# An S4 and mixture-of-experts block: filter tables made in 16 wide steps, expert chunks regrouped, and the last stage's loads issued by SyncE

## What is computed

```python
# s4: a long convolution per feature h, whose kernel comes from 64 complex modes
dtA  = exp(log_dt)[:, None] * A                       # [H, 64]
coef = C * (exp(dtA) - 1.0) / A
vand = exp(dtA[:, :, None] * arange(Lq))              # powers of exp(dtA)
kern = 2.0 * einsum('hn,hnl->hl', coef, vand).real    # [H, 4096]
y = irfft(rfft(xn) * rfft(kern))[:Lq]
z = gelu(y + xn * D) @ W_out + b_out                  # gated by a sigmoid half
# moe: 16 experts, every token through all, weighted by `combine` (2 nonzero of 16)
h  = silu(xn @ We1[e] + be1) * (xn @ We3[e] + be3)
yo = h @ We2[e] + be2
out = sum_e combine[:, e] * yo_e  +  shared expert
```

## Time and profile before

| | us |
|---|---|
| median of 2 runs | 10923.64 |
| the two runs | 10829.25 and 11018.03 |
| the profiled execution | 10848.99 |
| its span (core 5, the slowest) | 10847.4 |
| PE busy, of the span | 4786.6 (44%) |
| DVE busy | 4317.1 (40%) |
| ACT busy | 2336.4 (22%) |
| POOL busy | 2228.4 (21%) |

### The profile page before, as it was taken

The page is one execution under the profiler, slowest core; times in us unless marked ns, Lnnn a source line. Parts: engine busy times, 40 slices in busy tenths (PEclk is TensorE's granted clock), DMA queues, the critical chain, the costliest instruction groups (busy, mean ns, idle before and its releaser), DMA issues.

```text
span 10847.4 us, 92715 instructions; the slowest of 8 cores (10731.5 to 10847.4 us)
## 1 busy us (share of the span) xinstructions
PE 4786.6 (44%) x26752; PEld 2699.4 (25%) x26752; DVE 4317.1 (40%) x9126; ACT 2336.4 (22%) x3389; POOL 2228.4 (21%) x3656
## 2 busy tenths in 40 slices
PE   0000556666565555555433333323315554544541
PEld 0000222232222222222211111111114343433431
DVE  6244344444433343344355555544413232322322
ACT  1021333333333333333333333311100000000000
POOL 1000222333232223233222222200101111111110
PEclk9999777777777777777655555557657777777776
DMA  4500222222222222221111111110073435445347
GB/s 131 117 15 13 53 53 53 56 57 56 58 58 55 53 52 61 53 53 45 39 28 27 27 28 27 27 43 26 23 98 71 67 75 68 70 67 70 70 70 179
DMA packets 471658, 620.67 MB, mean 57 GB/s; under 512 B 285073, under 2 KB 330513, under 8 KB 470114
## 3 DMA queue, kind: packets, MB, share of 16 engines
q0 software_dynamic: 223152, 513.42, 23.4%
q1 hardware_dynamic: 144034, 75.11, 2.9%
q10 hardware_dynamic: 103968, 26.22, 1.5%
HBM read 389.99 MB, written 259.13 MB: 60 GB/s over the span
## 4 chain that ended last, share of the span: by engine, by line
PE 32%; DVE 24%; DMA 13%; ACT 10%; issue 8%; another core or an unknown queue 6%; POOL 4%; DVEq 1%; ACTq 1%; SPq 0%; POOLq 0%
PE PS L1363 9%; PE PS L1368 9%; PE PS L1550 8%; DMA p_h<-dH 5%; POOL dKLOC L920 3%; DVE p_h L1568 3%; PE PS L538 2%; DMA dH<-p_h 2%; DMA dKLOC<-p_xbuf 2%; ACT L1074 2%; ACT L548 2%; PE PS L1028 1%; DMA dP<-p_at 1%; DVEq L187 1%
## 5 line engine op out<-in xcount | busy, mean ns | idle before, releaser
L1550 PE MATMUL PS<-p_h,p_w 128*128 128x256 bf16 x8192 | 1142.8, 312 | 1226.2 <-DVE p_h L1574 1226.2
L1550 PEld LDWEIGHTS PS<-p_h,p_w 128*128 128x128 bf16 x8192 | 904.9, 112 | 1464.2 <-issue 1258.8
L1363 PE MATMUL PS<-xnF,p_w 128*128 128x512 bf16 x4608 | 1150.5, 395 | 102.0 <-ACT p_h L1391 102.0
L1368 PE MATMUL PS<-xnF,p_w 128*128 128x512 bf16 x4608 | 1096.3, 381 | 0.0
L1568 DVE SCALAR_TENSOR_TENSOR p_h<-p_h,sb_be_t,p_s 128x256 bf16<-128x256 bf16 x1024 | 496.0, 484 | 1157.9 <-DMA p_h<-dH 1072.1
L920 POOL DMA_DIRECT2D dKLOC<-p_xbuf x1024 | 599.1, 763 | 1615.6 <-ACT p_xbuf L552 1601.8
L561 DVE TENSOR_TENSOR p_tw<-p_gbuf,s_t1r 128x512 bf16<-128x512 bf16 x128 | 54.4, 425 | 2029.0 <-ACT p_gbuf L549 2029.0
L1499 POOL DMA_DIRECT2D p_s<-dS x272 | 206.0, 757 | 2211.4 <-PE PS L1550 2211.4
L538 PE MATMUL PS<-p_grb,s_s2wr 128*128 128x256 bf16 x256 | 74.9, 395 | 1319.0 <-DVE p_gib L566 1272.5
L1054 PE MATMUL PS<-s_i1a,p_ybuf 128*128 128x256 bf16 x512 | 208.3, 407 | 1012.6 <-DVE p_ybuf L1126 1012.6
L1363 PEld LDWEIGHTS PS<-xnF,p_w 128*128 128x128 bf16 x4608 | 465.0, 101 | 683.4 <-issue 174.3
(11 more groups left out here) (282 smaller groups left out, 8270.9 us busy)
## 6 DMA issues: line engine op xcount, KB each, us to landing
dS<-p_s POOLq DMA_DIRECT2D x576, 128.0 KB, 2.6
dH<-p_h POOLq DMA_DIRECT2D x576, 128.0 KB, 2.9
p_s<-dS POOLq DMA_DIRECT2D x256, 256.0 KB, 3.4
p_h<-dH POOLq DMA_DIRECT2D x256, 256.0 KB, 3.5
p_w<-we POOLq DMA_DIRECT2D x48, 1024.0 KB, 17.3
p_x<-x SPq DMA_DIRECT2D x64, 512.0 KB, 6.0
dKLOC<-p_xbuf POOLq DMA_DIRECT2D x1024, 32.0 KB, 2.0
p_k<-dKLOC POOLq DMA_DIRECT2D x512, 64.0 KB, 2.3
```

The costliest lines, as they stand in the source:

```text
L1363: ins = t.matmul(b1, w1b[u % 2][:, dc * 512 + ic * 128: dc * 512 + ic * 128 + 128], cx.xnF[:, dc * L + ts * 512: dc * L + ts * 512 + 512], ...
L1368: ins = t.matmul(b3, w3b[u % 2][:, dc * 512 + ic * 128: dc * 512 + ic * 128 + 128], cx.xnF[:, dc * L + ts * 512: dc * L + ts * 512 + 512], ...
L1550: ins = t.matmul(og, wsrc[:, ic * H + dc * 128: ic * H + dc * 128 + 128], buf[:, ic * 256:ic * 256 + 256], start=False, stop=(e == 16 and ...
```

## The change

Three edits.

1. Tables. The four small tables are made ahead of all groups, for all 1024 features, in 16 steps (4 blocks of 256 features x 4 tables). A step: SP loads six 64x256 float32 slices of `dWP`, DVE sets column 0 to 1 and 0 and runs the 18 products of the doubling at 256, 512 and 1024 elements, POOL stores real and imaginary table as bf16 in the new DRAM tensor `dF8`. SP and POOL wait for DVE, DVE for the loads and for the last step's stores. `P8` no longer starts from the coefficient; each group's build multiplies it in with six more operations, so a build has 18 operations of 64x2048 where there were 100 in all, and eight small loads of `dF8` by SP in place of one.
2. Chunks. Chunks 0 to 7 are emitted behind the table steps and ahead of the groups; the other 24 are spread over 32 groups, so that groups 0, 4, 8, ... 28 have none.
3. `emit_p6`. `she_load`, `abuf_load` and `cm6load` move from POOL's queue to SP's, in the same order; the weights and the `dM` store stay on POOL.

The diff, cut to its core:

```diff
+    D["dF8"] = nc.dram_tensor("dF8", [64, 8 * H * 8], BF16)
...
+            tabs = [(0, True, 0), (3, True, 2), (6, False, 4), (9, False, 6)]
+            nfb = 0
+            for c in range(4):
+                for (kbase, cj, pl) in tabs:
+                    @block.sync
+                    def _(sync, c=c, kbase=kbase, nfb=nfb):
+                        if nfb == 0:
+                            sync.wait_ge(swp.h, swp.val)
+                        else:
+                            sync.wait_ge(cv.h, cv.val)
+                        for st_ in range(3):
+                            k = kbase + st_
+                            sync.dma_start(out=mr3[:, st_ * 256:st_ * 256 + 256],
+                                           in_=dWP.ap()[(2 * k) * 64:(2 * k) * 64 + 64,
+                                                        c * 256:c * 256 + 256]).then_inc(sld2.h, 16)
...
+                    @block.vector
+                    def _(v, cj=cj, nfb=nfb):
+                        vo, vw = mkvo(cx, v)
+                        v.wait_ge(sld2.h, sld2.val)
+                        if nfb >= 1:
+                            v.wait_ge(sfb.h, 32 * nfb)
+                        vw(); vo(v.memset(ap(tbr, 0, [(2048, 64), (8, 256), (1, 1)]), 1.0))
+                        vw(); vo(v.memset(ap(tbi, 0, [(2048, 64), (8, 256), (1, 1)]), 0.0))
+                        for st_ in range(3):
+                            Tn = 2 ** st_
...
+                            vw(); vo(v.tensor_tensor(t1v, sr, wr_, ALU.mult))
+                            vw(); vo(v.tensor_tensor(t2v, si, wi_, ALU.mult))
+                            vw(); vo(v.tensor_tensor(dr, t1v, t2v,
+                                                     ALU.subtract if cj else ALU.add))
...
+                    @block.gpsimd
+                    def _(g, c=c, pl=pl):
+                        g.wait_ge(cv.h, cv.val)
+                        g.dma_start(out=ap(dF8, pl * 8192 + c * 2048, [(65536, 64), (1, 2048)]),
+                                    in_=tbr[:]).then_inc(sfb.h, 16)
...
+        for c5 in range(8):
+            p5_chunk(cx, st5, c5)
...
-            sync.wait_ge(swp.h, swp.val)
+            sync.wait_ge(sfb.h, sfb.val)
             for g_ in range(NKG):
                 if g_ >= 1:
-                    sync.wait_ge(cv.h, cv0 + (g_ - 1) * DVg + 100)
+                    sync.wait_ge(cv.h, cv0 + (g_ - 1) * DVg + 18)
                     sync.wait_ge(swk.h, swk.val)
-                src = ap(dWP, g_ * 32, [(1024, 64), (64 * 1024, 24), (1, 32)])
-                dst = ap(wkt, 0, [(24 * 32, 64), (32, 24), (1, 32)])
-                sync.dma_start(out=dst, in_=src).then_inc(swk.h, 16)
-                swk.val += 16
+                for pl, nm in enumerate(FPL):
+                    src = ap(dF8, pl * 8192 + g_ * 256, [(65536, 64), (1, 256)])
+                    sync.dma_start(out=BM[nm][:], in_=src).then_inc(swk.h, 16)
+                    swk.val += 16
...
+                sview = lambda t_: ap(t_, g_ * 32, [(H, 64), (1, 32), (0, 8), (0, 8)])
...
+                vw(); vo(v.tensor_tensor(tAv, bview("pr"), aview("wr"), ALU.mult))
+                vw(); vo(v.tensor_tensor(tBv, bview("pi"), aview("wi"), ALU.mult))
+                vw(); vo(v.tensor_tensor(tAv, tAv, tBv, ALU.subtract))
+                vw(); vo(v.tensor_tensor(tBv, bview("pr"), aview("wi"), ALU.mult))
+                vw(); vo(v.tensor_tensor(tCv, bview("pi"), aview("wr"), ALU.mult))
+                vw(); vo(v.tensor_tensor(tBv, tBv, tCv, ALU.add))
+                vw(); vo(v.tensor_tensor(tCv, sview(ucr), tAv, ALU.mult))
+                vw(); vo(v.tensor_tensor(tDv, sview(uci), tBv, ALU.mult))
+                vw(); vo(v.tensor_tensor(Ur[0:64, :], tCv, tDv, ALU.subtract))
...
-            p5_chunk(cx, st5, g_)
+            for c5 in range(8 + (g_ * 24) // 32, 8 + ((g_ + 1) * 24) // 32):
+                p5_chunk(cx, st5, c5)
...
-        @block.gpsimd
-        def _(g):
-            abuf_load(g, 0)
-            abuf_load(g, 1)
-            cm6load(g, 0)
-            cm6load(g, 1)
-            she_load(g, 0)
+        @block.sync
+        def _(sync):
+            quiesce(cx, sync, snap)
+            abuf_load(sync, 0)
+            abuf_load(sync, 1)
+            cm6load(sync, 0)
+            cm6load(sync, 1)
+            she_load(sync, 0)
...
+            @block.sync
+            def _(sync):
+                if ts + 1 < NTS:
+                    she_load(sync, ts + 1)
+                if ts + 2 < NTS:
+                    abuf_load(sync, ts + 2)
+                    cm6load(sync, ts + 2)
             @block.gpsimd
             def _(g):
-                if ts + 1 < NTS:
-                    she_load(g, ts + 1)
-                if ts + 2 < NTS:
-                    abuf_load(g, ts + 2)
-                    cm6load(g, ts + 2)
                 g.wait_ge(cv.h, evac_cv(ts))
```

More of the change, by code:

```diff
@@ L585, in emit_p2 @@
         ldt = S2_("p2_ldt", [1, H])
-        wkt = S2_("p2_wkt", [64, 24 * 32])
-        SM = {nm: S2_("p2s_" + nm, [64, 256]) for nm in
-              ["P8r", "P8i", "W8r", "W8i", "Q8r", "Q8i", "A8r", "A8i", "tp1", "tp2"]}
         BM = {nm: S2_("p2c_" + nm, [64, 256], BF16) for nm in
               ["pr", "pi", "wr", "wi", "qr", "qi", "ar", "ai"]}
-        t1 = S2_("p2_t1", [64, 2048], BF16)
-        t2 = S2_("p2_t2", [64, 2048], BF16)
+        tA = S2_("p2_tA", [64, 2048], BF16); tB = S2_("p2_tB", [64, 2048], BF16)
+        tC = S2_("p2_tC", [64, 2048], BF16); tD = S2_("p2_tD", [64, 2048], BF16)
         Ur = S2_("p2_Ur", [128, 2048], BF16)
@@ L769, in emit_p2 @@
         DAg = 4 + 16
-        DVg = 8 + 72 + 8 + 12 + 24
+        DVg = 18 + 24
         ct0 = ct.val
@@ L810, in _ @@
[L810 to L828, removed]
-                        if conj_tab:
-                            vw(); vo(v.tensor_tensor(di, tp1v, tp2v, ALU.add))
-                        else:
-                            vw(); vo(v.tensor_tensor(di, tp2v, tp1v, ALU.subtract))
@@ L833, in _ @@
-                dbl("P8r", "P8i", 0, True)
-                dbl("W8r", "W8i", 3, True)
-                dbl("Q8r", "Q8i", 6, False)
-                dbl("A8r", "A8i", 9, False)
-                for src_, dst_ in [("P8r", "pr"), ("P8i", "pi"), ("W8r", "wr"), ("W8i", "wi"),
-                                   ("Q8r", "qr"), ("Q8i", "qi"), ("A8r", "ar"), ("A8i", "ai")]:
-                    vw(); vo(v.tensor_copy(BM[dst_][:], SM[src_][:]))
                 bview = lambda t_: ap(BM[t_], 0, [(256, 64), (8, 32), (0, 8), (1, 8)])
@@ L855, in _ @@
-                vw(); vo(v.tensor_tensor(Vi[0:64, :], t1v, t2v, ALU.add))
+                sview = lambda t_: ap(t_, g_ * 32, [(H, 64), (1, 32), (0, 8), (0, 8)])
+                tAv = ap(tA, 0, [(2048, 64), (1, 2048)])
+                tBv = ap(tB, 0, [(2048, 64), (1, 2048)])
+                tCv = ap(tC, 0, [(2048, 64), (1, 2048)])
+                tDv = ap(tD, 0, [(2048, 64), (1, 2048)])
+                vw(); vo(v.tensor_tensor(tAv, bview("pr"), aview("wr"), ALU.mult))
+                vw(); vo(v.tensor_tensor(tBv, bview("pi"), aview("wi"), ALU.mult))
@@ new lines, in _ @@
+                vw(); vo(v.tensor_tensor(tCv, sview(ucr), tBv, ALU.mult))
+                vw(); vo(v.tensor_tensor(tDv, sview(uci), tAv, ALU.mult))
+                vw(); vo(v.tensor_tensor(Ui[0:64, :], tCv, tDv, ALU.add))
+                vw(); vo(v.tensor_tensor(tAv, bview("qr"), aview("ar"), ALU.mult))
+                vw(); vo(v.tensor_tensor(tBv, bview("qi"), aview("ai"), ALU.mult))
+                vw(); vo(v.tensor_tensor(Vr[0:64, :], tAv, tBv, ALU.subtract))
+                vw(); vo(v.tensor_tensor(tAv, bview("qr"), aview("ai"), ALU.mult))
@@ L856, in _ @@
+                vw(); vo(v.tensor_tensor(tBv, bview("qi"), aview("ar"), ALU.mult))
+                vw(); vo(v.tensor_tensor(Vi[0:64, :], tAv, tBv, ALU.add))
             @block.tensor
```

56 lines of the change are left out of this document (35 added, 21 removed).

## The result

The changed kernel takes 11469.7 us (median of 11 runs, 11397.1 to 11622.4); the kernel before, beside it, 10942.2 us (median of 10, 10800.1 to 11024.5). The ratio, taken like all ratios here over the executions that no lower clock held back, is 1.058 with a 95% interval of 1.054 to 1.062: 5.8% slower (the two medians, over all executions, divide to 1.048). The forecast was 11200 us, range 10950 to 11420: the sign was right, the size too small, and the time lies above the range. The profiled execution of the changed kernel took 11622.37 us; its slowest pair of cores, 0 and 1, was held at a lower clock than the rest. I therefore read core 5 for mechanisms and all eight cores for sizes.

What follows compares the result with a forecast made beforehand. No engine is full; FFTs and chunks in the filter stage, load waits and slice-end holes in the last stage set the time. 10849 + 587 (filter stage) − 237 (last stage) = 11199, say 11200 us; range 10950 to 11420.

Steps and rivals of the forecast that it cites:

- step (5): Boundaries between token slices in the last stage: eviction leaves the path, about 8 us for each of 14, −112 us.
- Step (4): Last stage's loads on SP: an expert pair's wait is 3.5 us in place of 4.27, −120 us in all.
- step (1): Tables ahead of the groups: 16 steps of 23.2 us that nothing hides, +310 us, less 14 run early.
- Step (2): Eight chunks at one stretch: cold starts save 12 us, lower clock costs 25, +13 us.
- Step (3): Groups' build takes 36.6 us; in 8 groups without a chunk TensorE waits 34.8 us each, +278 us.
- The filter stage as a whole: Tables, chunks and groups together: 310 − 14 + 13 + 278 = +587 us.
- Rival C: Last stage: the queue change buys only the sequencer's time, 38 us in all; 11275 us; chance 0.10.
- rival A: Last stage: combine-weight load quick on SP, boundaries 8 us, opening hole closes; 168 and 97 more, 10935 us; chance 0.15.

Runs made afterwards that it cites:

- e3: Changed kernel with every chunk back behind its own group, tables still made ahead: 11177 us, ratio 1.031 to the kernel before.
- e5: Changed kernel with the work of chunks 0 to 7 emitted 9 units behind each of the 16 table steps: 11225.8 us.
- b3: Kernel before, loads on POOL, with combine weights copied once into 128 DRAM rows and loaded from there: 10542.2 us, ratio 0.956 to the kernel before.
- b2: Kernel before with the last stage's loads on SP and combine weights copied into 128 DRAM rows: 10514.6 us.
- e1: Changed kernel with the `emit_p6` of the kernel before: 11653.7 us, ratio 1.058 to the kernel before.
- e2: Kernel before with the new `emit_p6`: 10822.9 us, ratio 0.993 to the kernel before.
- e6: Changed kernel with the 432 remaining chunk units spread 13 or 14 to each of the 32 groups: 11274.9 us.
- e9: Changed kernel with the six 64x256 loads of a table step made as two of 64x768: 11528.5 us.
- e8: Changed kernel with combine weights copied into 128 DRAM rows during groups 1 to 16 and loaded from there: 10990.7 us.
- e4: Changed kernel with the combine-weight load alone back on POOL's queue: 11718.6 us.

## Why the forecast was wrong

Of the 286 us by which the stages cost more than forecast, the largest piece is step (5): the boundaries brought nothing where 112 us were forecast. Step (4) lacks 60 and step (1) 54.

- *Step (1), a table step.* The term that failed first in time: 23.2 us predicted, 26.7 measured. The idle part was taken as the last load's latency behind six issues of 0.6 us (6.4); with the stores beside them SP's issues stretch to 1.9 us from the fourth on and the gap is 8.7, and with fewer loads the stores hold it at 7.75. The DVE part was 16.8 and is 17.8, by the 256-element products. 16 steps: +54 us. That nothing hides it was right (`e3`, `e5`).
- *Step (2), eight chunks at one stretch.* +13 was predicted, 25 of it for clock. From the end of the tables to the first build core 5 took 1945 - 1398 = 547 us; eight chunks at the 68 of before (a cycle of 4184 / 32 = 131 less 62.4), less the 14 run early and the 12 of cold starts, are 520: 27 us more, 5 of them between the tables' end and the first unit (1409). Clock is a part of it, and not the same on every core. The stretch from 1500 to 1900, core 1 and core 5 of the kernel after:

```profile
1500.00:1900.00 400.00, 380.92 (x1566) 162.88 (x1565) 0.00 (x0) 131.33 (x201) 110.64 (x202) 0.87 0.30 81
...
1500.00:1900.00 400.00, 362.15 (x1644) 162.02 (x1642) 0.00 (x0) 137.11 (x210) 116.80 (x212) 0.96 0.35 89
```

- *Step (3), the uncovered builds.* Right: 36.6 us predicted and 36.5 measured, the four products with a float32 broadcast at 2.28 us as assumed, 8 x 34.7 us of hole, and spreading the chunks gave 270 back.
- *The filter stage as a whole.* 562 without the clock's 25, 648 measured: 54 + 27 explain all but 5 of the difference. The other part of the +692 is clock, in which executions of the kernel before differ too (5219 to 5400 us among its cores).
- *Step (4), the loads on SP.* The mechanism held and the size was too large: a pair gained 0.5 us (4.27 to 3.75), not 0.8, because `p_h`, interpolated between a 64 KB and a 1 MB load at 2.9, lands in 3.3. In a slice that made 124 to 120 us, -60 in all instead of -120. With the slow load out of the way it is -91 (matmul spans of `b3` and `b2`: 1972 and 1881). More than half of the rest is in the first four experts of a slice: the move to SP gains 1.5 us there beside the slow load (28.0 to 26.5) and 2.7 without it (27.5 to 24.8). Through which wait was not followed. Rival C's price of 38 us was too low. The rule of the Trainium skill that it leans on (page "DMA: Bandwidth & Descriptors", section "Issuing engines are not separate DMA queues"), that starting transfers from several engines only saves issue time, is not quite what these rows show: the landing is sooner too (`p_s` 2.9 for 3.4, `p_h` 3.3 for 3.5).
- *Step (5), the boundaries.* The step that failed most: -112 predicted, about 0 measured. The order of events was as told, but the 8 us of a boundary were never won. Held against each other at like distance between the two neighbours' loads, the boundaries are 2.6 to 2.9 us longer than before (means, us; POOL: `before` and `e1`, SP: `after`, `e2`, `e3`, `e5`, `e6`, `e9`):

| loads issued apart by | landing, POOL | landing, SP | boundary, POOL | boundary, SP |
|---|---|---|---|---|
| 5 to 10 | 49.7 | 54.4 | 40.4 | 43.0 |
| 15 to 20 | 42.5 | 47.4 | 33.2 | 36.0 |
| 25 to 30 | 34.4 | 40.3 | 25.4 | 28.3 |

  From the landing to the next slice's first matmul the path is 3.1 us shorter (6.7 for 9.8), where 4.7 were forecast. But the load is not issued 3 us earlier: it goes out 18.3 us ahead of the slice's last matmul, for 19.0. And it lands some 5 us later after its issue, which the sum put at nothing. Why the slow load takes longer from SP is open.

  I also took `p_cmb` as a fixed 54.2 us from core 5's row. It was the row of the slowest pair. The load takes 30 to 62 us and goes with the distance to the neighbour's, so the drift between two cores moves the boundary by 20 us, up on one pair and down on another; and the slowest core, which sets the time, is drawn from four pairs. Over the five other runs with the new `emit_p6` the mean boundary lies between 31 and 37 us, for 34.6 and 34.2 in the two runs with the old one. The earlier trace rows had 29 us of wait on core 2 beside the 49 of the earlier trace rows on core 5: I used the difference to price rival A and did not ask what it came from.
- *Rival A* named the right place and the right price: once the load is quick, the boundaries are 8 us and the opening hole closes. From before to `e8` the last stage went from 219 + 2477 to 142 + 2017 us, 537 less, where the rival said 237 + 168 + 97 = 502. That the sums agree so well is partly luck: the slices gave 91 for 120, the 14 boundaries 368 for 280, the opening 77 for 102. Its condition was wrong: the move to SP did not make the load quick, it made it some 5 us slower; the change of source did.

## What to carry to other kernels

A DMA that broadcasts a small DRAM source to 128 partitions in short pieces should be priced from its own row, and of several cores, and be suspected first when its row shows many times the latency of another transfer of its size: here a copy into 128 rows, made in idle time, took 480 us off. A hole behind a slow transfer doesn't go away by changing its queue as long as the DMA engines are what it fills; the window's DMA share beside its GB/s (0.86 at 46, against 0.28 at 81) says so beforehand. And work that is made shorter on an engine that was covered brings nothing, while moving the cover away costs its whole length.

## What the runs showed of the hardware

- 1 MB in pieces of 512 bytes, each read 128 times from one place: 30 to 62 us, shorter the further apart the two neighbouring cores issue it; from 128 places: 8.9 us at any distance; 1 MB in pieces of 8 KB, each read 128 times: 6.9 to 9.2 us by core in `e8` (medians; 8 to 12 in `b2` and `b3`).
- While the slow load, issued by POOL, was under way in `e4`, no packet of SP's queue started for some 37 us after SP's issue at 10194.44.
- Cores 0/1, 2/3, 4/5 and 6/7 go together: in the time of that load, in the boundaries, and in the granted clock of a stretch (0.87 and 0.96 above on cores 1 and 5). The Trainium skill, page "TensorE: Matmul & The Clock Gate", section "Seeing it yourself", has one of its throttles act on a whole die; in these runs the lower clock struck pairs, different ones in each execution: in `e1` a granted clock of 0.81 stands on cores 0/1 for some 505 us between 3124 and 4934, on cores 2/3 of the same die for some 375 us between 7951 and 9760, and never on both pairs at once.
- SP issues six loads of 64 KB in a row in 0.45, 0.58, 0.58, 1.91, 1.45 and 1.08 us beside two stores of POOL, and in 0.45 to 0.58 each in the one step without them; two of 192 KB in 0.57 and 0.60 beside the stores.
- A float32 product of 64x256, operands 8 elements apart, takes 0.60 us, 64x512 0.68 and 64x1024 1.22. That the spacing is the cause of the first was not tested.
